# 448 unused bytes ahead of the normalised activations, in a gated-linear-attention and feed-forward layer on one Trainium2 core

## What is computed

```python
xn = layernorm(x)
# attention branch (cut): 256 -> 512 features
x_ = xn @ up_w.T;  gate = xn @ gate_w.T
shift = silu(conv4(x_) + conv_b)
q, k, g, tau = shift @ (q_w, k_w, g_w, tau_w).T          # 64 keys each
v = sigmoid(x_ @ ig_w1.T @ ig_w2.T + ig_b2) * x_
o = gla_chunk_scan(q * SCALE, k / |k| * softplus(g)**sigmoid(tau), v, decay)
o = rmsnorm((o + shift * residual) * silu(gate)) * norm_w
# feed-forward branch: 256 -> 1024 -> 1024 -> 1024 -> 256, ternary weights with a scale per output
h = silu(xn @ w1.T * s1) * (xn @ w2.T * s2)
h = gelu(h @ h1.T * sh1);  h = gelu(h @ h2.T * sh2)
out = x + o @ down_w.T + h @ w3.T * s3
```

## The kernel before

| Buffers | Start | mod 256 | mod 512 |
|---|---|---|---|
| `wwhole`, `whi`, `wlo` (pieces of 512 bytes) | 1,152, 91,264, 107,648 | 128 | 128 |
| `xin` (input and output) | 131,008 | 192 | 448 |
| `xnth`, `xntl`, `hid0h`, `hid0l`, `hid1h`, `hid1l` | 135,104 to 163,776 | 192 | 448 |
| `mixed`, `raw`, `xbuf` | 171,968 to 180,160 | 192 | 448 |
| `shift`, `parth`, `partl`, `sgate`, `zs`, `v`, `small`, `work`, `att`, `atth`, `attl`, `stateh`, `statel`, `kdq` | 184,320 to 225,280 | 0 | 0 |

## Time and profile before

### The profile page before, as it was taken

One profiled execution on the slowest core, in us unless ns is written; L12 is line 12 of the kernel. 1 busy time (PEld: TensorE's weight loads), 2 busy tenths in 40 slices (PEclk: granted clock), 3 DMA queues, 4 the chain that ended last, 5 costly groups with the idle time before them and its releaser, 6 DMA issues.

```text
span 2045.9 us, 46741 instructions
## 1 busy us (share of the span) xinstructions
PE 2025.3 (99%) x17478; PEld 2000.3 (98%) x17478; DVE 1575.3 (77%) x4242; ACT 1260.3 (62%) x2495; POOL 68.5 (3%) x104
## 2 busy tenths in 40 slices
PE   7999999999999999999999999999999999999998
PEld 7999999999999999999999999999999999999998
DVE  7787778877778877787877788777778777878776
ACT  5665656665556666566656566655566665666564
POOL 0000000000000000000000000000000000000000
PEclk9999999999999999999999999999999999999999
DMA  8000000000000000000000000000000000000000
GB/s 293 7 11 12 12 11 2 12 12 12 12 1 11 12 12 12 11 1 12 11 12 12 8 4 12 12 12 12 1 11 12 12 12 11 1 12 11 12 7 7
DMA packets 23360, 34.22 MB, mean 17 GB/s; under 512 B 2945, under 2 KB 19713, under 8 KB 23186
## 3 DMA queue, kind: packets, MB, share of 16 engines
q1 hardware_dynamic: 23186, 31.46, 4.6%
HBM read 23.07 MB, written 8.39 MB: 15 GB/s over the span
## 4 chain that ended last, share of the span: by engine, by line
PE 85%; DVE 5%; issue 5%; ACT 4%; SPq 1%; DMA 0%; DVEq 0%; POOLq 0%; POOL 0%; ACTq 0%
PE fb L355 56%; PE ab L355 23%; PE ab L563 2%; ACT raw L794 1%; PE ab L519 1%; PE ab L507 1%; PE ab L423 1%; ACT L787 1%; PE fb L641 1%; ACT hid0h L712 1%; DVE work L1049 0%; DVE raw L944 0%; DVE hid0l L930 0%; DVE v L1003 0%; ACT hid1h L712 0%
## 5 line engine op out<-in xcount | busy, mean ns | idle before, releaser
L355 PE MATMUL fb<-hid1h,wwhole 128*128 128x256 f32 x2048 | 493.3, 283 | 4.1 <-DVE hid1l L847 0.7
L355 PE MATMUL fb<-hid1l,wwhole 128*128 128x256 f32 x2048 | 485.4, 279 | 0.0
L355 PE MATMUL fb<-hid0h,wwhole 128*128 128x256 f32 x2048 | 483.9, 279 | 0.0
L355 PE MATMUL fb<-hid0l,wwhole 128*128 128x256 f32 x2048 | 483.9, 279 | 0.0
L355 PEld LDWEIGHTS fb<-hid1h,wwhole 128*128 128x128 f32 x2048 | 384.2, 188 | 11.7 <-issue 8.6
L355 PEld LDWEIGHTS fb<-hid1l,wwhole 128*128 128x128 f32 x2048 | 384.4, 188 | 0.0
L355 PEld LDWEIGHTS fb<-hid0l,wwhole 128*128 128x128 f32 x2048 | 384.2, 188 | 0.0
L355 PEld LDWEIGHTS fb<-hid0h,wwhole 128*128 128x128 f32 x2048 | 384.2, 188 | 0.0
L794 ACT ACTIVATE raw<-fb,sh_s 128x256 f32<-128x256 f32 x512 | 213.1, 467 | 208.1 <-PE fb L355 207.2
L355 PE MATMUL fb<-xnth,wwhole 128*128 128x256 f32 x1024 | 239.3, 277 | 0.0
L355 PE MATMUL fb<-xntl,wwhole 128*128 128x256 f32 x1024 | 239.1, 277 | 0.0
(11 more groups left out here) (212 smaller groups left out, 4641.7 us busy)
## 6 DMA issues: line engine op xcount, KB each, us to landing
xin<-x SPq DMA_DIRECT2D x32, 256.0 KB, 2.8
out<-xin SPq DMA_DIRECT2D x32, 256.0 KB, 2.2
stage_more<-stage_w SPq DMA_DIRECT2D x6, 512.0 KB, 7.2
sgate<-stage_w SPq DMA_DIRECT2D x4, 512.0 KB, 5.1
shift<-stage_w SPq DMA_DIRECT2D x4, 512.0 KB, 5.5
v<-stage_w SPq DMA_DIRECT2D x4, 512.0 KB, 5.8
raw<-stage_w SPq DMA_DIRECT2D x3, 512.0 KB, 6.0
mixed<-stage_w SPq DMA_DIRECT2D x3, 512.0 KB, 8.4
```

Source lines behind the costliest of these rows:

```text
L355: mm = pe.matmul(o, a, b, start=start and i == 0, stop=stop and i == len(pairs) - 1)
```

## The change

One buffer of 448 bytes for each partition, which nothing reads or writes, is laid between `xin` and `xnth`.

```diff
         xin = sb("xin", [P, HALVES, NC, H])
+        sb("spacing", [P, 112])
         xnth, xntl = sb("xnth", [P, HB, N], F32R), sb("xntl", [P, HB, N], F32R)
         hid0h, hid0l = sb("hid0h", [P, FB, N], F32R), sb("hid0l", [P, FB, N], F32R)
         hid1_place = next_place()
```

## The result

| | Before | After |
|---|---|---|
| median, beside each other | 2045.9 us (2045.21 to 2047.03) | 2072.91 us (2070.93 to 2073.38) |
| ratio, with its 95% interval | 1 | 1.0128 [1.0115, 1.0141] |
| span of the profiled execution | 2045.9 us | 2071.6 us |
| mean granted clock | 0.999 | 0.998 |

The change costs 27.0 us. It was forecast to cost 39.7, in a range that holds the result. In the profiled executions it is 25.7 us.

What follows compares the result with a forecast made beforehand. The prediction took TensorE, busy 99% of the span, as the bound: number of matmuls times the distance between starts. Terms +42.1 - 1.5 - 0.9 = +39.7 us on 2045.3 gave 2085 us, range 2041 to 2090.

Steps and rivals of the forecast that it cites:

- The mechanism: TensorE's matmul pace depends on the operands' start distance modulo 256; at distance 0 it would be the filler's 120.0 ns.
- The pace terms: 400 matmuls a half with `xnt*` or `hid*` slow to 120.0 ns, +42.1 us; 48 with `part*` gain, -1.5 us.
- the term for the wait: Hidden layer 2: wait timed from hidden layer 1's end; twelve slower matmuls eat 27 ns, -0.9 us, bound 0 to -2.
- The small terms: State update and outputs keep distance 0; VectorE and ScalarE show no visible cost of place.
- The loads: Start of kernel: loads go from remainder 0 to 192, covered by the filler; 0 to +1 us, taken as 0.
- A: TensorE matmuls: distance counts modulo 512, 256 is best, every stretch could run at 113.3 ns; 2002 us, chance 0.20 including partial.
- B: TensorE matmuls: only alignment to 128 bytes counts, all with both operands aligned run at 118.7 ns; 2068 us, chance 0.17.
- C: TensorE matmuls: place means nothing, paces belong to stages' orders and sizes; 2045 us, chance 0.13 including effects that cancel.

Runs made afterwards that it cites:

- s256: Kernel before with 256 unused bytes ahead of `xnth` in place of 448: 2047.60 us, ratio 1.0005.
- allmove: Kernel before with the 448 bytes laid ahead of the weights, so every buffer moves and all distances stay: 2046.92 us, ratio 1.0003.
- scan: Adds 44 runs of 24 filler matmuls at the start, moving operand 0 to 480 bytes further on in steps of 32: 120.0 ns at 0 and 256.
- short_before: Kernel before with the convolution's last tap on VectorE done for 128 of 256 tokens: 2033.26 us, ratio 0.9929.
- short_after: Changed kernel (448 bytes added) with the convolution's last tap done for 128 of 256 tokens: 2073.46 us, ratio 1.0124 to the kernel before.
- only_xnt: Kernel before with only `xnth` and `xntl` moved by 448 bytes, all behind by 512, so only they come to distance 0: 2054.27 us, ratio 1.0031.
- only_hid: Kernel before with only the four `hid*` buffers moved by 448 bytes, all behind by 512, so only they come to distance 0: 2066.98 us, ratio 1.0091.
- scan2: Adds 48 runs of filler matmuls at the start, distances 8 to 248 bytes in steps of 8 without multiples of 32: 113.3 ns at 112, slowest 122.5.
- d112: Kernel before with `xnt*`, `hid*` and `part*` at 240 modulo 256, distance 112 where they stream, 144 where weights stream: 2040.52 us, ratio 0.9964.

## Why the prediction was right, and where it was not

**The mechanism holds.** That the pace hangs on the distance of the operands modulo 256, and that the changed kernel would meet the filler's 120.0, is what the changed profile, `s256`, `allmove` and `scan` show. The pace terms were +42.1 and -1.5 us. By the starts they are 649 + 266 + 276 + 52 and some 27 behind the gate, 1270 ns a half or 40.6 us, and -34 ns or -1.1 us, 39.5 us together. `short_before` and `short_after` give 40.2, of which 2.7 is a wait.

**The step that failed** is the term for the wait, and one that is missing beside it. The prediction put the wait in hidden layer 2 down to parts "whose time runs from the end of hidden layer 1", counted twelve slower matmuls against it and took 0.9 us, at most 2. In truth the chain starts at the up projection, more than 250 matmuls earlier; those get over 900 ns longer, and the wait is 341 ns a half. So nearly all of it went: 282 ns, 9.0 us. The same chain feeds the input gate, where 156 of 159 ns went, 5.0 us; the prediction had no term for it. Together 14.0 us against 0.9, and 39.7 - 13.1 = 26.6 is near what was measured (27.0; 25.7 in the profiled executions). `only_xnt` shows the anchor, `short_before` the size of the waits, and `short_after` that the changed kernel has none of this kind left to give. The chain that the prediction had in mind, from the end of hidden layer 1, exists, but it was the shorter of two: it sets only the 58 ns a half that are left. That the range holds the result says little, for it reaches from 4 us faster to 45 us slower.

Both sizes could have been read before. The earlier trace rows names 0.7 us of waiting for `hid1l`, and I took this for the whole. It is a single wait, of the last sequence; those of the loop don't appear there, for a matmul's row lasts 0.28 us and the next is due 0.118 after its start, so a wait of up to some 160 ns is covered by the row before it, and of a longer one only the rest is idle time. Only the starts show it: 0.38 and 0.19 us at the seventh pair, in a stage whose neighbours I divided by their counts.

**The small terms.** State update, outputs, VectorE and ScalarE at 0: right; attention and small products together moved by 12 ns a half, 0.4 us. The loads: nothing beyond noise, the first half starts 51.9 us into the span where it was 51.6.

**The rivals.** A (modulo 512, 256 the best place) falls with 120.0 at distance 256, in the changed kernel and in `scan`. B (only alignment to 128) would have 118.7 everywhere; it falls with the same number, and with `scan`'s 120.0 at distance 96. C (place means nothing) falls with the result. The rule of the Trainium skill (SBUF — State Buffer, "SBUF: two separate sides") by which the two operands come through independent ports does not hold here as a rule for time: moving only the one costs 6.7 ns a matmul in the first 96, and moving both costs nothing. The chance of .67 for slower and the range, whose low end was drawn out to C, stood on these cases.

**What stays open.** Why a stretch at distance 64 or 192 takes 113.3 at one time and 117.8 at another. `only_hid` shows that the entry matters; the runs don't say what in it. Nor is it shown which accesses collide: the runs give times and addresses only.

## What to carry to other kernels

When TensorE is the bound, divide a stretch of starts by its count, and compare stages by where their operands lie: here 113.3 to 120.0 ns for the same shape, and choosing the places brought 0.5% for nothing. Before you cost a change of pace, find every wait of that engine from the distances of its starts, and follow each back to the point from which its chain runs without that engine; a slower engine gets such waits back first, and a faster one pays them first. Then look for the next chain behind it, which sets how much of the wait can go. To learn what a pace is worth, shorten the other side's work in both kernels and compare those two.

## What was unexpected of the hardware

- The pace of 256-column matmuls of this type at full granted clock ranges from 113.3 to 122.5 ns, with the distance of the operands' starts modulo 256, down to steps of 8 bytes (`scan`, `scan2`).
- At the same distance it has two values, 113.3 and 117.8, and an unchanged stretch can change from one to the other when what runs ahead of it changes (14 us in `only_hid`).
- A stationary operand that starts off a multiple of 64 bytes ran at 120.0 in both stages of `d112` that have one. No run separates that offset from the distance of 144 that both have.
